# Far attention scores from two key copies in 64-row products, layer-norm rows and state copies on ScalarE, and a new order, in a one-core attention, state-space and feed-forward kernel

## The reference

```
x = x + attention(ln(x))      # 16 heads of 8; a query sees the last 32 keys and every 64th key before
x = x + ffn(ln(x))            # 128 -> 512 -> 512 -> 128 with weights of +1 and -1, relu
x = x + mamba(ln(x))          # 256 inner channels, 16 states each, conv of 4, scan over 1024 steps
x = x + ffn(ln(x))            # the same ffn
# in mamba, per channel e, state n and step t:
h = exp(dt*A) * h + (dt*u) * B;   y = sum over n of h*C;   out = (y + u*D) * silu(z) @ W_out
```

## Time and profile before

| | us |
|---|---|
| median of 3 runs (811.11 to 813.23) | 812.72 |
| the profiled execution | 811.52 |
| its span in the profile | 809.7 |
| busy PE / DVE / ACT / POOL | 721.4 / 695.3 / 594.8 / 664.2 |

### The profile page before, as it was taken

One profiled execution on the slowest core, in us unless ns is written; L12 is line 12 of the kernel. 1 busy time (PEld: TensorE's weight loads), 2 busy tenths in 40 slices (PEclk: granted clock), 3 DMA queues, 4 the chain that ended last, 5 costly groups with the idle time before them and its releaser, 6 DMA issues. The chain is left out here.

```text
span 809.7 us, 22189 instructions
## 1 busy us (share of the span) xinstructions
PE 721.4 (89%) x7840; PEld 430.6 (53%) x7840; DVE 695.3 (86%) x1187; ACT 594.8 (73%) x1161; POOL 664.2 (82%) x824
## 2 busy tenths in 40 slices
PE   5999988998789999998999999899896889897887
PEld 3765655644455447545555456355452356453566
DVE  6977229999999989999889999999998989799983
ACT  5776698797788989887689978868667744764533
POOL 5143437998899989989999799899998999999961
PEclk9999999999999999999999999999999999998999
DMA  5000019888799668877777889889797899898950
GB/s 200 3 3 2 2 54 269 226 231 229 206 225 237 159 173 238 230 177 200 198 213 197 225 233 243 232 230 244 207 253 199 252 259 240 215 266 235 264 158 27
DMA packets 84177, 154.94 MB, mean 191 GB/s; under 512 B 9433, under 2 KB 10082, under 8 KB 84066
## 3 DMA queue, kind: packets, MB, share of 16 engines
q1 hardware_dynamic: 84066, 153.51, 71.4%
HBM read 142.46 MB, written 11.01 MB: 190 GB/s over the span
## 5 line engine op out<-in xcount | busy, mean ns | idle before, releaser
L1779 POOL TENSOR_TENSOR d<-d,cr 128x1024 f32<-128x1024 f32 x128 | 300.0, 2354 | 13.8 <-DVE d L1279 4.1
L1578 ACT ACTIVATE ps<-dt,An 128x512 f32<-128x512 f32 x256 | 173.7, 690 | 71.9 <-DVE d L1279 60.5
L1279 DVE TENSOR_TENSOR_SCAN d<-ps,hl,d 128x512 f32<-128x512 f32 x128 | 157.0, 1262 | 3.7 <-ACT ps L1578 3.3
L1279 DVE TENSOR_TENSOR_SCAN d<-ps,d 128x512 f32<-128x512 f32 x128 | 149.6, 1202 | 7.2 <-ACT ps L1578 6.5
L1267 DVE TENSOR_TENSOR d<-ps,d 128x512 f32<-128x512 f32 x184 | 118.5, 671 | 7.1 <-DMA d<-dud 7.1
L891 PE MATMUL ps<-h,w 128*128 128x512 f16 (+1 forms) x512 | 114.3, 373 | 3.5 <-DVE h L1224 2.8
L1766 POOL TENSOR_TENSOR d<-d,br 128x512 f32<-128x512 f32 x72 | 91.5, 1277 | 4.3 <-DMA d<-dud 4.3
L891 PEld LDWEIGHTS ps<-h,w 128*128 128x128 f16 x512 | 46.8, 98 | 70.9 <-DVE h L1224 12.8
L966 PE MATMUL ps<-d,cst 128*32 128x512 f32 x512 | 69.3, 614 | 10.6 <-POOL d L1779 6.4
L1434 ACT COPY pt<-ps 128x512 f32<-128x512 f32 x96 | 53.8, 589 | 13.9 <-PE ps L825 10.6
L825 PE MATMUL ps<-cst,sx 128*128 128x128 f32 x384 | 56.3, 281 | 8.0 <-ACT sx L1427 3.5
(11 more groups left out here) (182 smaller groups left out, 1457.1 us busy)
## 6 DMA issues: line engine op xcount, KB each, us to landing
dt<-dtd SPq DMA_DIRECT2D x256, 256.0 KB, 5.3
d<-dud SPq DMA_DIRECT2D x256, 256.0 KB, 4.8
dtd<-sR SPq DMA_DIRECT2D x16, 256.0 KB, 4.4
dud<-sE SPq DMA_DIRECT2D x16, 256.0 KB, 3.8
X<-in_x SPq DMA_DIRECT2D x8, 256.0 KB, 6.3
br<-bcd SPq DMA_DIRECT2D x8, 256.0 KB
cr<-bcd SPq DMA_DIRECT2D x8, 256.0 KB
out<-X SPq DMA_DIRECT2D x3, 512.0 KB, 5.8
```

What stands on the lines that cost most here:

```text
L1279: eng.tensor_tensor_scan(d, banks[u % NG][:, :], d, hl[:, r:r + 1] if m % 2 else 0.0, ALU.mult, ALU.add).then_inc(v_sc, 1)
L1578: eng.activation(banks[u % NG][:, :], DT[:, u % NT, :], ACT.Exp, scale=An[:, g:g + 1]).then_inc(s_da, 1)
L1779: eng.tensor_tensor(d, d, CR[m % 2][:, :].unsqueeze(1).to_broadcast((128, n, 512)), ALU.mult).then_inc(p_cm, n)
```

## The change

- **Far scores in pairs.** A unit is now (kind, g, kk, c), with c the half of the heads, for far units too. `KD` has two copies of the keys (even and odd 32-row blocks), made by a multiplication with `rmask` over 128 rows, two instructions for four. `asc_t` makes two units at once from 64 contraction rows each: two mask products, then 2x8 products of 64 key columns (far) or 2x4 of 128 key columns (near; before 16 in 64x64 blocks).
- **Rows, X update and last states by ACT.** ACT writes all four normalized rows, but for `aln` of (0,1) and the first two feed-forward passes (`SHARED`). The X update is a step of its own on ACT, `mxu_s`. The copy to `hl` is a step of ACT, `hl_s`, and `out_p` waits for it.
- **Places.** All numbers of `PLACES` and `WARM` are new: 36 groups of dummy products with 238 products, before 28 groups with 152. Which units' inputs are driven by POOL (`DRIVEN_P`) is unchanged.

```diff
-UNITS = [(kind, g, kk) for kind, g in GROUPS for kk in range(2 if kind else 4)]
+UNITS = [(kind, g, kk, c) for kind, g in GROUPS for kk in range(1 if kind else 2) for c in range(2)]
...
+SHARED = FFN_ORDER[:2]
...
-        KD = sb("KD", [128, 4, PAD + T])
+        KD = sb("KD", [128, 2, PAD + T])
...
-                    for k in range(4):
-                        m = 8 * g + 4 * kk + k
-                        lq = qm[:, 4 * kk + k, :, :].rearrange("p a n -> p (a n)")
-                        t = eng.matmul(bw[:, :, k, :].rearrange("p a (h x) -> p a h x", x=4), lq, Ks[:, :, :, 4 * m:4 * m + 4], start=False,
-                                       stop=(k == 3 and u not in SHIFTED_T), skip_group_check=True)
...
+                half = [slice(64 * c, 64 * c + 64) for c in range(2)]
+                two = []
+                for c in range(2):
...
+                    eng.matmul(bank[:, :], e4[half[c], :], mk, start=True, stop=False, skip_group_check=True)
...
+                for k in range(nw):
...
+                        lq = qm[half[c], wi, :, :].rearrange("p a n -> p (a n)")
+                        dst = two[c][:, :, k, :]
+                        if kind:
+                            rk, dst = Ks[half[c], :, :, 4 * m:4 * m + 4], dst.rearrange("p a (h x) -> p a h x", x=4)
+                        else:
+                            at = 64 * (m % 16) + m // 16
+                            rk = KD[half[c], :, at:at + 127:2]
+                        t = eng.matmul(dst, lq, rk, start=False, stop=(k == nw - 1 and u + c not in SHIFTED_T), skip_group_check=True)
...
-                for a in range(4):
-                    t = eng.copy(KD[32 * a:32 * a + 32, a, PAD + h:PAD + T:2], bank_of["aqk", b, h, 1][32 * a:32 * a + 32, :])
+                for a in range(2):
+                    t = eng.activation(KD[:, a, PAD + h:PAD + T:2], bank_of["aqk", b, h, 1][:, :], ACT.Identity, scale=rmask[:, a:a + 1])
...
-                for k in range(n // 2):
+                for k in range(n // 2 if f in SHARED else n):
...
-                for k in range(2):
+                if m:
+                    eng.wait_ge(t_md, 2 * m)
+                    eng.wait_ge(l_bc, 16 * m)
+                for k in range(4):
...
+            def mxu_s(m):
+                c1, r1p = mr[:, 3, :], mr[:, 5, :]
+                eng.wait_ge(s_mno, m + 1)
+                eng.wait_ge(p_mrs, 7 * m + 7)
+                for k in range(4):
+                    xk = X[:, 4 * m + k, :]
+                    t = eng.activation(xk, xk, ACT.Identity, bias=c1[:, k:k + 1], scale=r1p[:, k:k + 1])
+                t.then_inc(s_mxa, 1)
...
+            def hl_s(u):
+                r = u % NR
+                eng.wait_ge(v_sc, u + 2)
+                eng.copy(hl[:, r:r + 2], D[:, u % ND:u % ND + 2, 511]).then_inc(s_hl, 2)
...
-                for k in (2, 3, 0, 1):
-                    if k == 0:
-                        eng.wait_ge(s_mno, m + 1)
-                    t = eng.tensor_scalar(X[:, x0 + k, :], X[:, x0 + k, :], r1p[:, k:k + 1], c1[:, k:k + 1], ALU.mult, ALU.add)
-                t.then_inc(p_mxa, 1)
...
-                    eng.tensor_scalar(hl[:, r:r + 2], d[:, :, 511], 1.0, 0.0, ALU.mult, ALU.add).then_inc(p_hl, 2)
-                    eng.wait_ge(p_hl, NR * (m // 2) + r + 2)
+                    eng.wait_ge(s_hl, NR * (m // 2) + r + 2)
```

More of the change, by code:

```diff
@@ L170 @@
     (PAIRS, 'out_p'),
+    ([(u,) for u, in PAIRS if u // NR % 2 == 0], 'hl_s'),
 ]
 PLACES = {
[L175 to L188, removed]
[5 rows of a table removed]
@@ L531, in hybrid_block @@
         PT = [sb(f"pt{i}", [128, 4, 128]) for i in range(2)]
-        ZF = [sb(f"zf{i}", [128, 4, 4, 16]) for i in range(3)]
+        ZF = [sb(f"zf{i}", [128, 8, 2, 16]) for i in range(3)]
         ZN = [sb(f"zn{i}", [128, 8, 4, 9]) for i in range(2)]
@@ L789, in asc_t @@
-                if g == 2:
-                    eng.wait_ge(p_kp, b + 1)
-                for k in range(4):
-                    m = 8 * g + 4 * kk + k
-                    at = 64 * (m % 16) + m // 16
-                    for c in range(2):
-                        r = slice(64 * c, 64 * c + 64)
-                        for j in range(2):
-                            o = slice(64 * j, 64 * j + 64)
-                            lq = qm[r, 4 * kk + k, 2 * j:2 * j + 2, :].rearrange("p a n -> p (a n)")
-                            dst = two[c][o, :].rearrange("p (a w k) -> p a w k", a=2, w=4)[:, :, k, :]
-                            t = eng.matmul(dst, lq, KD[r, 2 * c:2 * c + 2, at:at + 127:2], start=False,
-                                           stop=(k == 3 and u + c not in SHIFTED_T), skip_group_check=True)
-                        if k == 3:
+                Ks = KD[:, :, PAD:PAD + T].rearrange("p a (h x) -> p a h x", x=128)
@@ L1350, in ano_s @@
                 eng.wait_ge(p_ars, 4 * (2 * b + h + 1))
-                for k in range(4 * h, 4 * h + (2 if b or h else 4)):
+                for k in range(4 * h, 4 * h + (2 if (b, h) == (0, 1) else 4)):
                     t = eng.activation(LNA[:, k, :], X[:, 8 * b + k, :], ACT.Identity, bias=rs[:, 1, k:k + 1], scale=rs[:, 0, k:k + 1])
@@ L1361, in aqk_s @@
                         return
-                    eng.wait_ge(p_set, 3)
-                    for a in range(4):
-                        t = eng.copy(KD[32 * a:32 * a + 32, a, PAD + 1:PAD + T:2], bank_of["aqk", b, 1, 1][32 * a:32 * a + 32, :])
+                    for a in range(2):
+                        t = eng.activation(KD[:, a, PAD + 1:PAD + T:2], bank_of["aqk", b, 1, 1][:, :], ACT.Identity, scale=rmask[:, a:a + 1])
                     t.then_inc(s_aqk, 1)
@@ L1445, in aown_s @@
                 else:
-                    kk, c = near(u)
                     z = ZN[g % 2][:, 4 * kk:4 * kk + 4, 2 * c:2 * c + 2, :]
@@ L1451, in aown_s @@
                 eng.wait_ge(t_pv, U + 1)
-                eng.copy(z, bank_of["pv", b, u][:, 0:144 if kind else 72].rearrange("p (w a n) -> p w a n", w=4, n=9)).then_inc(s_own, 1)
+                eng.copy(z, bank_of["pv", b, u][:, 0:144 if kind else 72].rearrange("p (w a n) -> p w a n", a=2, n=9)).then_inc(s_own, 1)
             def jexp_s(b, g):
@@ L1611, in aln_p @@
                     eng.wait_ge(s_ano, 2 * b + h - 1)
-                    eng.wait_ge(p_ano, 2 * b + h - 2)
+                    if b == 1:
+                        eng.wait_ge(p_ano, 1)
                 eng.wait_ge(v_aag, 8 * b + 4 * h + 4)
                 scales("a", 4 * h, p_ars, 4 * (2 * b + h))
-                if h == 0 and b:
-                    eng.wait_ge(t_av, 8 * (b - 1) + 4)
+                if (b, h) != (0, 1):
+                    return
                 eng.wait_ge(p_ars, 4 * (2 * b + h + 1))
-                if b == h == 0:
-                    return
-                for k in range(4 * h + 2, 4 * h + 4):
+                for k in range(6, 8):
                     t = normal(LNA[:, k, :], X[:, 8 * b + k, :], "a", k)
```

358 lines of the change are left out of this document (179 added, 179 removed), and 324 rows, old and new, of tables (PLACES, WARM).

## The result

The changed kernel took 889.92 us (median of 4 runs, 885.67 to 893.86) against 812.98 us for the kernel before on the same chip (811.11 to 814.44): a ratio of 1.0945, 95% interval 1.0893 to 1.0998. The prediction was 805.2 with a range of 793 to 820, so its size and its sign are both wrong. The profiled execution has a span of 883.9 us (809.7 before).

A forecast was written before the change was run, and what follows sets the result against it. No single bound in the scan stage: DVE and POOL fullest, POOL setting the pace from 641 to 722 us; PE before it. Start -2, stage -5.9, end +0.4 give -7.5, so 805.2 us, range 793 to 820.

The forecast's parts named there:

- the stage's sum: Scan stage, 130 to 784 us: -6.9 at m=6, -4 elsewhere, +5 taken back by ACT, -5.9 us in all.
- Elsewhere ... somewhat under half of it I give to the change: Scan stage outside 641 to 722 us: of 9.2 us of DVE's waits for transfers and POOL, -4 us is won.
- The five rivals: More won (0.20), nothing measurable (0.14), ACT waited for (0.18), dummy products in the way (0.05), row halves not overlapping (0.03).
- Together 61 us: POOL's work taken away by moving copies (21.8), X update (13.9) and rows; about 57 us of it in the stage.
- so POOL falls to some 84% and stops being a bound: Scan stage: POOL, at 93% before, loses about 57 us of work and no longer sets the pace.
- DVE's idle time falls to the share of the other stretches: At m=6, 641 to 722 us: DVE idles 5.2 us instead of 12.1, a gain of 6.9 us.
- +44 us: ACT's added work from rows, X update and copies, less fewer key copies; 41 us of it in the stage, reaching 82%.
- ACT becomes the one waited for: Rival, chance 0.18: slower through late decays in the stage's first half; 824 us if waits for ACT double.
- The far pair: PE, two far units at once: 16 steps at 0.11 plus 0.27 for masks, 2.05 us, 0.17 less than before.
- The near pair: PE, two near units at once: 8 steps at 0.11 plus masks, 1.16 us, 0.44 less than before.
- forecast 2 earlier: Start, before the first scan: -3 us from attention pairs on PE, +0.9 from ACT's rows; bounds -4 and +2.
- nothing measurable: Rival, chance 0.14: 810.3 to 815.1 us, since DVE bounds all but one stretch and ACT returns what POOL gives.

The follow-up runs named there:

- e6: Code of the kernel before with the changed kernel's places and dummy-product list, odd far unit right behind its even one: 907.54 us (1.117).
- e18: Changed kernel with POOL's product with C cut to 8 of 512 columns in the even half batches: 813.02 us (0.997).
- e20: Changed kernel with POOL's product with C cut to 8 of 512 columns in the odd half batches instead: 888.69 us (1.091).
- e1: Changed kernel with the copies to `hl` back on POOL in `out_p`, places as in the change: 880.37 us (1.083).
- e3: Kernel before, own places, with only the copies to `hl` moved to ACT, as late against its decays as in the change: 822.42 us (1.012).
- e8: Kernel before, own places, with only the rows and the X update moved to ScalarE: 832.62 us (1.025).
- e10: Changed kernel in its new places, with rows, X update and last-state copies back on POOL, so the pairs alone: 902.36 us (1.111).
- e19: Kernel before with POOL's product with C cut to 8 of 512 columns in the even half batches: 810.70 us (0.995).
- e9: Kernel before, own places, with the copies to `hl` made by VectorE one of its steps behind the scan: 835.54 us (1.029).

## Why the prediction was wrong, point by point

**The step that failed** is the stage's sum, -5.9 us. It let every moved piece of work be worth its duration where it stands and took the new places as costing nothing: "Elsewhere ... somewhat under half of it I give to the change". The order got no term. "if the new places shift DVE work to where another engine is full; the rows of before can't show the last" stood under what would make it wrong, with no chance of its own among the rivals. The five rivals were about pieces of work, none about the order of the list. The runs put 95 us on the list (e6) and tie the 77 us between the kernels to one wrong duration in it (e18 to e20). No row of before could give that size, but the table could show the fault: 0.19 between two products beside rows of 2.36. Nor did the table promise a gain, with its last scan 8 us later than before.

**POOL.** "Together 61 us": busy time fell from 664 to 609 us, 55, and by 48 in the stage where 57 were forecast. Of the 61, 9 are the gaps behind the copies (64 x 0.14), which no busy time holds; against that 4 us of fills for the halved `KD`, ahead of the stage, were left out of the sum. "so POOL falls to some 84% and stops being a bound" was right. "DVE's idle time falls to the share of the other stretches" was not: at m=6 it was to be 5.2 us and is 30.1 (97.50 - 67.42).

**ACT.** +44 us were forecast, and 29 measured (595 to 624). By their own lines the rows take 34.6 us more, forecast 38.7, and the copies 10.7, forecast 12.8. All lines together grow by 37; the total grows by less, since neighbouring instructions overlap. The copy takes 0.19 us, forecast 0.20. A key copy takes 0.74 us and not 0.62, so -6.7 and not -7.4 there. DVE's waits for ACT grew from 23.4 us in all to 42.8 in the four largest rows, of which the scans' waits for decays are 23.4 (9.8 in the earlier trace rows):

```profile
DVE sT L1243 <- ACT sE L1555: 7.3, 8, 2.5
DVE h L1209 <- ACT h L1469: 6.8, 5, 3.9
...
DVE h L1215 <- ACT h L1477: 5.3, 8, 0.8
```

That is past the 36 us at which the rival *ACT becomes the one waited for* was to decide. It has a true core: copies late on ScalarE cost 10 us (e1, e3) and the rows in the old order 20 (e8), where the scans wait 23.0 us for decays as well:

```profile
DVE d L1282 <- ACT ps L1593: 23.0, 26, 2.6
```

But in e18, with the same work on ScalarE, that row has 7.7 us and the 77 us are gone, so the waits for ACT in the changed kernel were mostly another face of the order:

```profile
DVE d L1271 <- ACT ps L1580: 7.7, 10, 2.3
```

**PE.** The far pair was forecast at 2.05 us and takes 2.05, with 16 steps at 0.11 (1.83 / 16). The Trainium skill (TensorE: Matmul & The Clock Gate, LDWEIGHTS (loading the stationary operand)) makes that an estimate of 1.7 us at two loads at a time. The total agrees within a tenth, its parts do not: a load is 0.191 us long in the trace and not 0.107, and 1024 of them fill 66.6 us, 0.065 each, so nearly three are under way at once. The near pair was forecast at 1.16 and takes 1.40. The term mis-sized is its step: 8 steps in 1.13 us (344.09 - 342.96), 0.14 each, and not 0.11. In time the pairs are worth 5 us at most in the new order (e6 to e10), and not clearly that.

**Dummy products.** 61.3 us against 40.8, +20.5 where +23 was forecast. Whether they were in the way was not measured apart. e18 has them all and takes 813.

**Start and end.** The first scan starts 4.1 us later (133.9 against 129.8), forecast 2 earlier. This too comes with the order: in e6, the old code in it, the first scan starts at 137.1, in e10 with the pairs at 134.4. The rows on ScalarE in the old order put it at 132.1 (e8). The end is 26.2 us against 25.8, +0.4 as forecast.

**What it would have been.** Where the order's durations are made true by leaving work out, the changed kernel stands at the time of the kernel before with the same work left out: 813.0 and 810.7 us (e18, e19). If that carries over to a kernel with all its work, it would have been the rival *nothing measurable*; no run shows it. An order made with 2.36 us for the product, the one kernel that could beat both, was not tried. No kernel here beats the one before with all of its work done.

**What stays open.** The runs show that the loss goes when the wrong duration is made true, and only in the half batches that have it, and that neither the ring `D`, the copies nor the place of product or sum alone carries it. They do not show which positions in the five lists turn 139 us of unplanned work, on an engine that idles 24 to 33 us in these half batches, into some 55 us there. The waits after m=0 go round through copy, product, sum, transfer and drive, and removing one station moves the wait to the next.

## What to carry to other kernels

A change that comes with a new hand-set order is two changes: run the old code in the new order and the new code in the old order before explaining anything by the work that moved. If the order's numbers are times, compare the gap behind each kind of step with its duration in the trace; a step with a twelfth of its real length shows at once. Where one ring of buffers is made deeper, look whether the next ring in the same queue takes over the wait. And a long wait in a circle of engines that wait for each other is no cause until taking it away gives time: here POOL's longest wait, 54.8 us, was worth 10 us, and it was 74.2 in the kernel that was fast.

## What the runs showed of the hardware

- A copy of 128x2 fp32 takes 0.19 us on ScalarE, 0.19 on POOL (64 copies, 12.3 us), and on VectorE 0.13 to 0.17 us in 34 of 64 cases (e9).
- In the other 30 cases VectorE's copy took 0.27 to 2.90 us, and 28 of them ended within 0.03 us of the end of a two-input fp32 operation of POOL that was under way. The 6 copies that lay wholly beside a one-input operation of POOL or one of 4 columns took 0.13 to 0.17 us.
- TensorE's granted clock was lower where PE waited more: 0.87 at m=4 in the changed kernel, 0.98 before and 0.96 in e18. PE's busy time there is 72.0 us, 70.9 before, so the lower clock explains little of the loss; m=0 and m=2 grew by 9 and 14 us at 0.98 and 0.97.
- Weight loads of 64x128 fp32 in two row halves overlapped nearly three deep: 1024 loads fill 66.6 us, 0.065 each, though one lasts 0.19.
